# Stack attention: norms of q and k in two passes, row sums one slot later, mask product in eight tiles

## What is computed

```
def attn_layer(x, Wqkv, qs, ksc, Wo):
    q, k, v = split(x @ Wqkv)               # 16 heads of 64
    q = l2norm(q) * qs ;  k = l2norm(k) * ksc
    q = q * cos * scale + rotate_half(q) * sin * scale
    k = k * cos / scale + rotate_half(k) * sin / scale
    # each window of 32 queries sees its own 32 keys and the 32 before;
    # mask: (it < jb) | (it > jb + 32) | (jb == -1)
    sim = where(mask, -max, q k^T * 8)
    out = softmax(sim) @ v
    return out @ Wo
def ffn_layer(x, ...):
    return a * gelu(gate) @ W2 + b2         # a, gate = split(layernorm(x) @ W1 + b1)
for i in range(6):
    x = attn_layer(shift_tokens(x), ...) + x
    x = ffn_layer(shift_tokens(x), ...) + x
```

## Time and profile before

| | us |
|---|---|
| median of 3 runs | 4362.35 |
| lowest, highest | 4358.89, 4362.66 |
| the profiled execution | 4365.13 |
| its span | 4363.3 |

### The profile page before, as it was taken

The page is one execution under the profiler, slowest core; times in us unless marked ns, Lnnn a source line. Parts: engine busy times, 40 slices in busy tenths (PEclk is TensorE's granted clock), DMA queues, the critical chain, the costliest instruction groups (busy, mean ns, idle before and its releaser), DMA issues. The chain is left out here.

```text
span 4363.3 us, 151598 instructions
## 1 busy us (share of the span) xinstructions
PE 3866.2 (89%) x66488; PEld 2314.4 (53%) x66488; DVE 3296.5 (76%) x4385; ACT 2534.1 (58%) x3236; POOL 2498.8 (57%) x2036
## 2 busy tenths in 40 slices
PE   6887799999999999999778877899999999999997
PEld 3323456665665666665433334566666666666664
DVE  7997777888888787888454436788888878878884
ACT  6885456566665666666324444556566565666654
POOL 0001677777777777777100005786777777777773
PEclk8999999999999999999789998999999999999998
DMA  0001232332323233222000002323323223232221
GB/s 19 1 1 42 72 87 65 85 77 75 83 67 87 73 78 85 62 67 62 17 1 1 1 14 74 92 62 84 81 67 85 73 79 80 73 81 71 66 60 40
DMA packets 165593, 260.83 MB, mean 60 GB/s; under 512 B 58572, under 2 KB 79816, under 8 KB 164936
## 3 DMA queue, kind: packets, MB, share of 16 engines
q1 hardware_dynamic: 164936, 251.13, 22.2%
HBM read 48.61 MB, written 1.05 MB: 11 GB/s over the span
## 5 line engine op out<-in xcount | busy, mean ns | idle before, releaser
L1374 POOL TENSOR_TENSOR f_k_rotated<-f_rope_ak,f_rope_bk 128x1024 f32<-128x1024 f32 x192 | 454.5, 2367 | 288.7 <-DVE f_rope_bk L1429 288.7
L1097 PE MATMUL banks<-f_wqkv,H 128*128 128x512 f32 x1152 | 564.9, 614 | 17.4 <-DVE f_E L1469 9.2
L1097 PE MATMUL banks<-f_wqkv,G 128*128 128x512 f32 x1152 | 551.8, 601 | 0.0
L1426 DVE TENSOR_TENSOR f_rope_aq<-banks,f_rope 128x1024 f32<-128x1024 f32 x192 | 235.1, 1225 | 389.5 <-ACT f_sqq L1284 376.2
L1361 POOL MEMSET f_kT<- 128x256 f32 x2 | 0.6, 311 | 839.9 <-POOLq L514 460.5
L1374 POOL TENSOR_TENSOR f_q_rotated<-f_rope_aq,f_rope_bq 128x1024 f32<-128x1024 f32 x192 | 454.5, 2367 | 29.0 <-DVE f_rope_bq L1429 28.6
L1319 ACT ACTIVATE f_V<-banks 128x1024 f32<-128x1024 f32 x192 | 196.8, 1025 | 418.7 <-PE banks L1097 418.3
L1152 PEld LDWEIGHTS banks<-f_O_T,f_wo 128*128 128x128 f32 x3072 | 372.6, 192 | 98.3 <-issue 94.6
L1152 PE MATMUL banks<-f_O_T,f_wo 128*128 128x128 f32 x3072 | 375.4, 275 | 6.4 <-issue 5.2
L1392 POOL TENSOR_TENSOR f_E<-f_E,f_row_inverse 128x1024 f32<-128x1024 f32 x192 | 368.6, 1920 | 19.8 <-DVE f_row_inverse L1484 19.8
L1386 POOL TENSOR_TENSOR f_q_rotated<-f_q_rotated,f_inverse_norm 128x1024 f32<-128x1024 f32 x192 | 365.2, 1902 | 15.0
(11 more groups left out here) (207 smaller groups left out, 8961.6 us busy)
## 6 DMA issues: line engine op xcount, KB each, us to landing
f_P_T_paired<-f_P_T SPq DMA_DIRECT2D x1536, 64.0 KB
f_V_previous<-f_V SPq DMA_DIRECT2D x192, 384.0 KB, 3.7
f_V_previous<-f_V SPq DMA_DIRECT2D x192, 128.0 KB, 2.4
f_wqkv<-in_L_ffn_Wqkv SPq DMA_DIRECT2D x48, 384.0 KB, 4.1
f_rope<-in_rope SPq DMA_DIRECT2D x24, 512.0 KB, 5.1
f_wo<-in_L_ffn_Wo SPq DMA_DIRECT2D x12, 512.0 KB, 5.4
f_w<-in_L_ffn_W SPq DMA_DIRECT2D x12, 341.0 KB
f_w<-in_L_ffn_W SPq DMA_DIRECT2D x24, 64.0 KB
```

Source lines behind the costliest of these rows:

```text
L1097: mm = nc.tensor.matmul(ps[:, o * BLK:(o + 1) * BLK], xs, w[:, c * INNER + o * BLK:c * INNER + (o + 1) * BLK], start=True, stop=True)
L1374: nc.gpsimd.tensor_tensor(qk[i][:], ra[i][:], rb[i][:], ALU.add).then_inc(radd.sem, 1)
L1426: nc.vector.tensor_tensor(heads_of(ra[i][:]), src, table(2 * i, 0, DH), ALU.mult).then_inc(rot.sem, 1)
```

## The change

1. The norm of q and the norm of k are made apart. `sums` clamps its own half (128x16). ACT seeds q directly after the squares of k, and k after the exp. POOL does, for q and then for k: rope addition, seed wait, four Newton steps on 128x16, multiplication.
2. DVE's sum of squares of q moves from behind the subtraction to between the rope of q and the rope of k.
3. Row sum and reciprocal, and POOL's multiplication of E with it, move from the end of slot s (tile n-1) to the head of the next slot (they serve tile n-2 there). DVE's transposes of P of n-2 move from between the ropes to behind the sum of squares of k. On SP the two V transfers now go ahead of the eight P transfers.
4. The mask is written by eight matmuls of 64 rows and 32 columns, 512 columns wide each, in place of two full ones.

The core of the diff:

```
@@ SP
+                if live(s):
+                    sp.wait_ge(v_ev.sem, v_ev.at(n))
+                    sp.wait_ge(o_mm.sem, o_mm.past(n - 3))
+                    sp.dma_start(Vp[n % 3][0:W, :], V[(n - 1) % 4][P - W:P, :]).then_inc(vp_in[n % 3].sem, 16)
+                    sp.dma_start(Vp[n % 3][W:P, :], V[n % 4][0:P - W, :]).then_inc(vp_in[n % 3].sem, 16)
                 if live(s - 2):
                     sp.wait_ge(ppt.sem, ppt.at(n - 2))
...
@@ PE
-                for i in range(2):
-                    nc.tensor.matmul(PT_S[:, i * BLK:(i + 1) * BLK], ident16[:],
-                                     mask[:, (1 if t else 0):(2 if t else 1), :].to_broadcast([P, HP, 2 * W]),
-                                     start=True, stop=False)
+                for g in range(NG):
+                    v = 1 if t or g else 0
+                    for i in range(2):
+                        rows = slice(i * DH, (i + 1) * DH)
+                        nc.tensor.matmul(PT_S[g * W:(g + 1) * W, i * BLK:(i + 1) * BLK], ident16[rows, i * DH:i * DH + W],
+                                         mask[rows, v:v + 1, :].to_broadcast([DH, HP, 2 * W]), start=True, stop=False)
@@ ACT
+            def seeds(n, i):
+                h = slice(i * HEADS, (i + 1) * HEADS)
+                act.wait_ge(clamped.sem, clamped.at(n, i + 1))
+                act.wait_ge(newton.sem, newton.past(n - 1, 4 * (i + 1)))
+                nc.scalar.activation(lg[:, h], ss[n % 2][:, h], ACT.Ln).then_inc(seeded.sem, 1)
...
                     squares(n, 1, k_mm, PK)
+                    seeds(n, 0)
...
-                    nc.scalar.activation(y0[:], lg[:], ACT.Exp, scale=-0.5).then_inc(seeded.sem, 1)
+                    seeds(n, 1)
@@ constants
     band[0:W, 0, 0:W] = NEG
+    band[2 * W:3 * W, 0, 0:W] = NEG
```

More of the change, by code:

```diff
@@ L1056, in _ @@
                     continue
[L1057 to L1060, removed]
                 l = layer(s)
@@ L1284, in squares @@
                 nc.scalar.activation(sq[i][:], ps, ACT.Square).then_inc(sqd.sem, 1)
+            def seeds(n, i):
[3 more added lines that the diff above has]
+                nc.scalar.activation(lg[:, h], ss[n % 2][:, h], ACT.Ln).then_inc(seeded.sem, 1)
+                act.wait_ge(seeded.sem, seeded.at(n, 2 * i + 1))
+                nc.scalar.activation(y0[:, h], lg[:, h], ACT.Exp, scale=-0.5).then_inc(seeded.sem, 1)
             ln_act(act)
@@ L1380, in _ @@
[L1380 to L1387, removed]
-                            .then_inc(nrm.sem, 1)
@@ new lines, in _ @@
+                        pool.wait_ge(newton.sem, newton.at(n, 4 * i + 1))
+                        nc.gpsimd.tensor_tensor(rt[:, h], rt[:, h], ss[n % 2][:, h], ALU.mult).then_inc(newton.sem, 1)
+                        pool.wait_ge(newton.sem, newton.at(n, 4 * i + 2))
+                        nc.gpsimd.tensor_scalar(rt[:, h], rt[:, h], -0.5, 1.5, ALU.mult, ALU.add).then_inc(newton.sem, 1)
+                        pool.wait_ge(newton.sem, newton.at(n, 4 * i + 3))
+                        nc.gpsimd.tensor_tensor(rn[:, h], rt[:, h], y0[:, h], ALU.mult).then_inc(newton.sem, 1)
@@ L1394, in _ @@
+                        pool.wait_ge(newton.sem, newton.at(n, 4 * i + 4))
+                        pool.wait_ge(radd.sem, radd.at(n, i + 1))
+                        nc.gpsimd.tensor_tensor(heads_of(qk[i][:]), heads_of(qk[i][:]), over(rn[:, h], DH), ALU.mult)\
+                            .then_inc(nrm.sem, 1)
                 if (b := feed(s, 8)) is not None:
@@ L1436, in sums @@
                     .then_inc(red.sem, 1)
+                dve.wait_ge(red.sem, red.at(n, i + 1))
+                h = ss[n % 2][:, i * HEADS:(i + 1) * HEADS]
+                nc.vector.tensor_scalar(h, h, 1e-24, None, ALU.max).then_inc(clamped.sem, 1)
             def gated(b, j, bk):
@@ L1454, in _ @@
                 n = tile(s)
+                if live(s - 2):
+                    dve.wait_ge(expd.sem, expd.at(n - 2))
+                    nc.vector.tensor_reduce(rs[:], by_side(E[n % 2]).rearrange("p b h w -> p h b w"), AX.XY, ALU.add)\
+                        .then_inc(smd.sem, 1)
+                    dve.wait_ge(smd.sem, smd.at(n - 2))
+                    dve.wait_ge(pn.sem, pn.past(n - 3))
+                    nc.vector.reciprocal(ri[:], rs[:]).then_inc(rid.sem, 1)
                 if live(s):
                     rotate(s, 0, q_mm, PQ)
-                if live(s - 2):
-                    dve.wait_ge(pn.sem, pn.at(n - 2))
-                    dve.wait_ge(pair_in[(n - 3) % 2].sem, pair_in[(n - 3) % 2].past((n - 3) // 2))
-                    nc.vector.transpose(PT[:].rearrange("p b t -> p (b t)"), E[n % 2][:]).then_inc(ppt.sem, 1)
+                    sums(n, 0)
                 if live(s):
@@ L1473, in _ @@
                 if live(s):
-                    sums(n, 0)
                     sums(n, 1)
-                    dve.wait_ge(red.sem, red.at(n))
-                    nc.vector.tensor_scalar(ss[n % 2][:], ss[n % 2][:], 1e-24, None, ALU.max).then_inc(clamped.sem, 1)
-                if live(s - 1):
-                    dve.wait_ge(expd.sem, expd.at(n - 1))
-                    nc.vector.tensor_reduce(rs[:], by_side(e).rearrange("p b h w -> p h b w"), AX.XY, ALU.add)\
-                        .then_inc(smd.sem, 1)
-                    dve.wait_ge(smd.sem, smd.at(n - 1))
-                    dve.wait_ge(pn.sem, pn.past(n - 2))
-                    nc.vector.reciprocal(ri[:], rs[:]).then_inc(rid.sem, 1)
+                if live(s - 2):
+                    dve.wait_ge(pn.sem, pn.at(n - 2))
+                    dve.wait_ge(pair_in[(n - 3) % 2].sem, pair_in[(n - 3) % 2].past((n - 3) // 2))
+                    nc.vector.transpose(PT[:].rearrange("p b t -> p (b t)"), E[n % 2][:]).then_inc(ppt.sem, 1)
                 if (b := feed(s, 8)) is not None:
```

26 lines of the change are left out of this document (10 added, 16 removed).

## The result

| | median us | lowest, highest | ratio to before, 95% interval |
|---|---|---|---|
| before (13 runs beside it) | 4362.66 | 4358.52, 4369.81 | |
| changed kernel (13 runs) | 4348.64 | 4340.71, 4352.25 | 0.9964 [0.9955, 0.9972] |

What follows compares the result with a forecast made beforehand. Bound by PE plus its wait for a chain ending in POOL (normalised q and k). 4365 (profiled) - 260 + 33 + 32 - 19 = 4151, less 2.8 to the median: 4148 us, -4.9%; range 4105 to 4270.

Steps and rivals of the forecast that it cites:

- The second clamp 0.1 to 0.2 to DVE: On DVE: separate clamps for q and k add only 0.1 to 0.2 us, hidden in idle time ahead of the ropes.
- 1.21, 0.03 between dependent instructions, 0.10 until the next can start: On DVE between the ropes: durations of q's sum and clamp, pushing the rope of k by 0.28 us.
- The waits for q and k: PE's waits for POOL's normalised q and k at the transposes: 260 us to win, 33 us of losses staying.
- I am wrong if k waits stay in kind 1 and 3: Sign of failure: PE's k waits of 0.5 us or more remaining in slots of kinds 1 and 3.
- The new wait for the copy of V: Kind 3 slots: q's seeds delay ACT's V copy, PE's hidden products wait 0.66 us in 48 slots, +32 us.
- The mask: PE's mask block ahead of the scores: eight small tiles save 0.1 us a slot, -19 us (ends -38 and +232).
- slow loads at 0.6 us a slot: Mask weight loads without fast load, one behind another: 115 us in all, sum near 4265; left out of the forecast.
- The rival of tiles one behind another: Mask tiles on PE run serially: +1.2 instead of -0.1 us a slot, 4398 us; chance of slower 0.05.
- the P transfer was in time: On SP: P transfer behind the V transfers still reaches the products in time, with 11.1 us available.
- margin of 3 us: Slack claimed for the P transfer before the products, from 11.1 us available, 6.60 us transfer and 1.6 us V transfers.
- Half is given back: Rival: POOL's chain late in kinds 1 and 3 through exp and variance behind the V copy; 4244 us, chance 0.22.
- The late P transfer: Rival: queueing on SP makes the P transfer 12.2 us, each slot loses 1.0 us; 4340 us, chance 0.05.

Runs made afterwards that it cites:

- experiment 1: Changed kernel with the two clamps of the sums as a tensor_reduce maximum over pairs of sum and floor, in place of tensor_scalar; 4162.71 us, ratio 0.9539.
- experiment 7: Kernel of experiment 1 with ACT's seeds of q behind the copy of V and the table load in slots with a gelu; 4304.71 us, ratio 0.987.
- The fastest kernel here: Kernel of experiment 1, eight-tile mask, with SP's loads of the next layer's weights and tables moved ahead of the P transfer; 4130.19 us, ratio 0.9471.

## Why the prediction was wrong

- **The duration of the clamp is the step that failed.** "The second clamp 0.1 to 0.2 to DVE" and the clamp inside "1.21, 0.03 between dependent instructions, 0.10 until the next can start". Both take the duration from the earlier trace rows, where POOL idles, for a place where POOL is in the addition that the same rope releases. Measured: 0.94 us on average, 384 times. By experiment 1 this costs 186 of the 200 us, up to (44 - 14) / 2 = 15 of them (an estimate) by the clock, which fell beside PE's longer standstills. The forecast put q's clamp right behind the rope whose end starts POOL's 2.36 us addition; had it laid beside the earlier trace rows at the new place, the overlap was there to see. That such an overlap costs time, the trace before showed in only 12 of its 192 clamps: they ran into POOL's addition and took up to 0.30.
- **The waits for q and k: right.** -260 + 33. With the clamp in a form that does not wait, k keeps 14.4 us, and q trades POOL for 22.8 us behind DVE's addition, 37 against the 33 left standing. "I am wrong if k waits stay in kind 1 and 3" did not happen: the 21 waits for k of experiment 1 lie in a stack's first slots, in its last, in slot 10 and in the first slot of a layer.
- **The new wait for the copy of V: right in kind and size**, 32 us forecast, 27.7 in experiment 1; 77.8 in the changed kernel, since the seeds wait for the long clamp as well.
- **The mask: block right, effect wrong.** It gained 0.2 us a slot where 0.1 was forecast, and was counted as if all of it reached the end. Measured: +8, +17, +3 and -3 us with the small tiles, on four bases. The Trainium skill (TensorEngine Tiling (Array Packing), Restrictions and Gotchas) says that column tiling excludes fast weight load, and the forecast had priced slow loads at 0.6 us a slot. No such cost is seen: the weight loads of the small tiles took 0.09 us each, those of the full ones 0.10, and the eight tiles took 0.23 together. The rival of tiles one behind another fell with it.
- **SP: the P transfer was in time** as forecast (PE waited for it twice, 4.8 us in all). The forecast's 6.60 us for it ended at a row whose bracket names DVE's write of H and not the transfer, so the margin of 3 us was weakly founded. And the weight loads, which stood behind it in the same queue, were not looked at. Their new place costs 27 to 32 us.
- **Sum.** Without the mask the forecast's terms give 4167; the kernel with a clamp that does not wait and the old mask gives 4160 with the loads' stalls and 4133 without them. The gain on this chain was forecast at 195 us and measured at 204 and 228 against before. The first of these is close in part by luck, since the loads' stalls, which no term had, take some 27 us off it. The mechanism was right; the missing thing was a rival, "an instruction that moves beside another engine's changes its own duration".
- **The rivals.** "Half is given back", 4244, named a late exp and variance as the cause, not the clamp. The late P transfer stood at 4340, near the measured 4348 by luck alone: PE's wait for that transfer, which it rests on, did not come.

## What to carry to other kernels

A duration belongs to a form of instruction and to a place: before a VectorE instruction moves, look at what GpSimd does there, and write small fp32 SBUF operations beside GpSimd in a form that doesn't wait (here a maximum by tensor_reduce, 186 ns against 936). A piece of work saved ahead of a wait for another engine is lost in that wait. The order of two edits matters as well: the row sum gave 52 us once PE no longer waited for the norms, and no gain was seen before that. A longer standstill of PE can cost twice, by itself and by the clock behind it. Where a "part alone" is tried, look for what else its edit puts on the chain. When a step moves in a queue, cost all that stands behind it there, weight loads too.

## What the runs showed of the hardware

- A 128x16 clamp on VectorE takes 0.17 to 1.87 us in one and the same kernel: where a GpSimd instruction is in progress at its start, it ends 0.03 to 0.08 us behind that one. tensor_scalar and tensor_tensor from SBUF do it, tensor_reduce (0.19 throughout) does not.
- Eight bf16 matmuls of 64 rows, 32 columns and 512 moving columns, in eight positions, take 0.23 us to the first score; two full ones 0.52.
- PE stood still for 2 us amid 128 small matmuls without any wait in the trace, at a DMA share of 0.05; moving six loads, issued 6.0 to 2.3 us ahead of them, to 1.3 to 4.2 us behind their end, and the other loads likewise, took 32 us off the kernel and the stalls of the ten slots behind such loads from 22.0 to 1.5 us.
- Beside standstills of PE of over 2 us for k the granted clock fell to 0.50 (1.2 GHz) for 3.4 us in 34 steady slots of experiment 7. A projection of four matmuls then took 3.38 in place of 1.81. It did not fall at every such standstill (8 of 42 longer than 1.5 us had none).
- The fastest kernel here, complete in its computation, took 4130 us, 5.3% less than before.
